# Loading a decoder kernel's weights first: the small parameters wait behind eight weight pieces, and the first activations are fetched inside the setup

## The reference

```python
x = _layernorm(x + _L0_attn_ref(x, ...))       # attention through 16 "splat" centres per head
x = _layernorm(x + _L0_xattn_ref(x, ctx, ...)) # attention to 120 context tokens
x = _layernorm(x + _L0_ffn_ref(x, ...))        # best one of 8 experts, 256 x 256 each
x = _layernorm(x + _L1_attn_ref(x, ...))       # causal attention
x = _layernorm(x + _L1_xattn_ref(x, ctx, ...)) # two attention blocks, each with a 256-1024-256 MLP
x = _layernorm(x + _L1_ffn_ref(x, ...))        # best 4 of 16 experts of 64 hidden features
```

## Time and profile before

| | |
|---|---|
| time, median of 3 runs | 3904.42 us (3902.85 to 9488.8; the middle one of the three is the median) |
| the profiled execution | 3903.38 us, its span 3901.6 us |
| PE busy | 3338.3 us, 86% of the span |
| DVE busy | 2759.7 us, 71% |
| ACT busy | 2093.8 us, 54% |
| POOL busy | 971.6 us, 25% |
| first instruction of the PE | 71.51 us after the start of the span |

### The profile page before, as it was taken

How to read it: one execution, slowest core, us unless ns; L and a number is a source line. 1 busy time by engine, 2 the same in 40 slices (tenths; PEclk the granted TensorE clock), 3 DMA queues, 4 the chain that set the end, 5 groups by cost and what they waited for, 6 DMA issues and landing times. The chain is left out here.

```text
span 3901.6 us, 94561 instructions
## 1 busy us (share of the span) xinstructions
PE 3338.3 (86%) x38960; PEld 2367.8 (61%) x38960; DVE 2759.7 (71%) x6299; ACT 2093.8 (54%) x4222; POOL 971.6 (25%) x1792
## 2 busy tenths in 40 slices
PE   1899888988898888988988888899888898988886
PEld 1666565666565656656656666576656665755654
DVE  5777676777776767767767667677776677767655
ACT  4745565455556564554465555545555556455552
POOL 0312341122222321131133122212342112124310
PEclk9989898989899989989889888899988998988887
DMA  5000000000000000000000000000000000000000
GB/s 165 3 3 2 2 3 5 9 8 3 2 2 3 6 3 7 7 3 2 7 2 2 5 4 8 5 4 2 2 2 3 10 9 4 2 2 2 1 4 6
DMA packets 30365, 31.49 MB, mean 8 GB/s; under 512 B 8673, under 2 KB 26482, under 8 KB 29938
## 3 DMA queue, kind: packets, MB, share of 16 engines
q1 hardware_dynamic: 29938, 25.44, 2.1%
HBM read 21.24 MB, written 4.19 MB: 7 GB/s over the span
## 5 line engine op out<-in xcount | busy, mean ns | idle before, releaser
L1113 ACT ACTIVATE p<-bank,p_log 128x512 f32<-128x512 f32 (+2 forms) x1280 | 746.5, 583 | 1299.2 <-PE bank L805 1242.7
L1687 POOL TENSOR_TENSOR prob<-p,prob 120x256 f16<-120x256 f32 (+2 forms) x512 | 452.4, 884 | 1746.5 <-ACT prob L1114 1745.0
L1114 ACT ACTIVATE prob<-bank,p_log 128x512 f16<-128x512 f32 (+2 forms) x1280 | 746.8, 583 | 0.0
L1389 DVE TENSOR_REDUCE negm<-bank 128x2 f16<-128x512 f32 (+1 forms) x1280 | 674.5, 568 | 30.5 <-PE bank L760 19.4
L1307 DVE TENSOR_TENSOR prob<-p,prob 128x512 f16<-128x512 f32 (+2 forms) x768 | 469.6, 618 | 181.8 <-ACT prob L1114 177.1
L782 PE MATMUL bank<-q,k 32*128 32x256 f16 (+2 forms) x6144 | 491.0, 286 | 59.2 <-issue 20.1
L672 PE MATMUL bank<-w_exp,ident_h 128*128 128x512 f16 x1280 | 426.6, 418 | 20.9 <-DVE k L1328 8.5
L1696 POOL TENSOR_SCALAR_AFFINE_SELECT probm<-prob 128x128 f16<-128x128 f16 x1024 | 325.6, 359 | 335.4 <-DVE prob L1307 335.1
L782 PEld LDWEIGHTS bank<-q,k 32*128 32x128 f16 (+1 forms) x6144 | 306.1, 109 | 137.4 <-issue 55.6
L805 PE MATMUL bank<-ident_h,negm 128*128 128x256 f16 (+2 forms) x2560 | 379.0, 270 | 0.0
L850 PE MATMUL bank<-v,prob 128*128 128x17 f16 (+2 forms) x8448 | 328.3, 174 | 33.3 <-DVE prob L1307 20.7
(11 more groups left out here) (302 smaller groups left out, 6254.8 us busy)
## 6 DMA issues: line engine op xcount, KB each, us to landing
x<-in_x SPq DMA_DIRECT2D x16, 256.0 KB, 2.7
out<-z SPq DMA_DIRECT2D x16, 256.0 KB, 2.2
xa<-in_li SPq DMA_DIRECT2D x9, 256.0 KB, 4.2
x<-in_li SPq DMA_DIRECT2D x7, 256.0 KB, 4.6
z<-in_wq SPq DMA_DIRECT2D x4, 256.0 KB, 4.1
z<-in_li SPq DMA_DIRECT2D x4, 256.0 KB, 4.6
cx<-in_ctx_t SPq DMA_DIRECT2D x16, 60.0 KB, 2.2
cx<-in_ctx SPq DMA_DIRECT2D x16, 60.0 KB, 1.8
```

Of the source, the lines that this page charges most:

```text
L1113: act(p32[0:n, g % PBUF32, 0:cols], ps[0:n, 0:cols], ACT.Exp, bias=p_log[0:n, :], scale=a.scale)
L1114: act(prob[0:n, 0, g % PBUF, 0:cols], ps[0:n, 0:cols], ACT.Exp, bias=p_log[0:n, :], scale=a.scale).then_inc(a_done, one(a_done))
L1389: v.tensor_reduce(negm[:, h * NT:(h + 1) * NT], ring_v[bank_of(e, v_full)][:, :].rearrange("p (t n) -> p t n", t=NT)[:, :, 0:ATTNS[k].keys ...
L1687: g.tensor_tensor(prob[0:n, 1, m % PBUF, 0:cols], p32[0:n, m % PBUF32, 0:cols], prob[0:n, 0, m % PBUF, 0:cols], ALU.subtract).then_inc(pp_ ...
```

## The change: pieces first, constants in the middle, x inside the setup

Four things are changed, all of them in the setup block or at the seam between the blocks:

1. SP issues weight pieces 0 to 7 first, then the 18 parameters of group 0 (now `needed`), then the rest of the pieces. The 17 of group 1 (`needed_later`) are issued one behind every second piece, from piece 8 to piece 40.
2. ACT makes the high parts of pieces 0 to 7 before it waits for group 0 and runs the two `exp`. DVE makes the low parts of pieces 0 to 7 before the constants.
3. The buffers are assigned from the end: piece n uses buffer (n - 61) % 8, so that the last pieces in `x` are 53, 54 and 55 and not 56, 57 and 58.
4. The first three `x` and context transfers are issued at the end of the setup's SP program, each `x` as soon as `low_made` says that its buffer is free, and not after the barrier.

No computing instruction is added or taken away. The diff, cut:

```diff
-        buffers = x + xa + z
+        def place_of(n):
+
+            return (n - len(chunks)) % STAGING
...
-                load(e, 0, cen[:, 0], io["centers"].rearrange("(t p) d -> p t d", p=P))
...
-                for n, (_, src, tiles, cols) in enumerate(chunks):
-                    if n >= STAGING:
-                        e.wait_ge(low_made, n + 1 - STAGING)
-                    e.dma_start(staging(n, tiles, cols), src).then_inc(staged[n % STAGING], 16)
+                def stage(n):
+                    _, src, tiles, cols = chunks[n]
+                    if n >= STAGING:
+                        e.wait_ge(low_made, n + 1 - STAGING)
+                    e.dma_start(staging(n, tiles, cols), src).then_inc(staged[place_of(n)], 16)
...
+                for n in range(STAGING):
+                    stage(n)
+                for dst, src in needed:
+                    load(e, 0, dst, src)
+                for n in range(STAGING, len(chunks)):
+                    stage(n)
+                    if needed_later and n % 2 == 0:
+                        load(e, 1, *needed_later.pop(0))
+                for dst, src in needed_later:
+                    load(e, 1, dst, src)
+                for b in range(LANES):
+                    e.wait_ge(low_made, len(chunks) - STAGING + LANE[b] + 1)
+                    e.dma_start(x[LANE[b]][:, :, :], io["x"][b].rearrange("(t p) f -> p t f", p=P)).then_inc(
+                        x_in[LANE[b]], 16)
+                for b in range(LANES):
+                    e.dma_start(cxT[LANE[b]], io["ctx_t"][b]).then_inc(c_in[LANE[b]], 16)
...
-                e.wait_ge(w_ready[0], w_count[0])
-
-                nc.scalar.activation(s_small[:, 6:10], s_small[:, 0:4], ACT.Exp).then_inc(s_act, 1)
-                nc.scalar.activation(s_small[:, 10:11], s_small[:, 4:5], ACT.Exp, scale=-1.0).then_inc(s_act, 1)
                 for n, (parts, _, tiles, cols) in enumerate(chunks):
-                    e.wait_ge(staged[n % STAGING], 16 * (n // STAGING + 1))
+                    if n == STAGING:
+                        e.wait_ge(w_ready[0], w_count[0])
+                        nc.scalar.activation(s_small[:, 6:10], s_small[:, 0:4], ACT.Exp).then_inc(s_act, 1)
...
                 for n, (parts, _, tiles, cols) in enumerate(chunks):
-                    e.wait_ge(staged[n % STAGING], 16 * (n // STAGING + 1))
+                    if n == STAGING:
+                        constants()
+                    e.wait_ge(staged[place_of(n)], 16 * (n // STAGING + 1))
                     e.wait_ge(high_made, n + 1)
...
-                for b in range(LANES):
-                    fetch_x(b)
-                for b in range(LANES):
-                    fetch_ctx_t(b)
```

More of the change, by code:

```diff
@@ L400, in spread_row @@
             return ap.rearrange("(a n) -> a n", a=1).broadcast_to([P, ap.shape[0]])
-        buffers = x + xa + z
+        def place_of(n):
+            return (n - len(chunks)) % STAGING
         def staging(n, tiles, cols):
-            flat = buffers[n % STAGING][:, :, :].rearrange("p a b -> p (a b)")
+            flat = (x + xa + z)[place_of(n)][:, :, :].rearrange("p a b -> p (a b)")
             return flat[:, 0:tiles * cols].rearrange("p (a b) -> p a b", b=cols)
@@ L451, in _ @@
-                load(e, 1, r_route[:, :], spread_row(io["route"]))
+                def stage(n):
[3 more added lines that the diff above has]
+                    e.dma_start(staging(n, tiles, cols), src).then_inc(staged[place_of(n)], 16)
+                needed = [
+                    (cen[:, 0], io["centers"].rearrange("(t p) d -> p t d", p=P)),
+                    (cen[:, 1], io["centers_t"].rearrange("(t p) d -> p t d", p=P)),
+                    (dlt[:, 0], io["deltas"].rearrange("(t p) d -> p t d", p=P)),
+                    (dlt[:, 1], io["deltas_t"].rearrange("(t p) d -> p t d", p=P)),
+                    (s_small[:, 0:2], io["log_scales"]),
+                    (s_small[:, 2:4], io["log_amps"]),
+                    (s_small[:, 4:5], spread_row(io["movement"])),
+                    (s_small[:, 5:6], spread_row(io["temperature"])),
+                    (p32[0:EXPERTS, 1, 0:DM], io["expert_b"])]
@@ new lines, in _ @@
+                for r, name in enumerate(("bo2", "li1_b0", "li1_b1", "li3_b0", "li3_b1")):
+                    needed.append((p32[BROW + r:BROW + r + 1, 0, 0:DM], io[name].rearrange("(a n) -> a n", a=1)))
+                for a in range(2):
+                    for c, name in enumerate(("ln_g", "ln_b")):
+                        needed.append((p32[GROW + a:GROW + a + 1, 0, c * DM:(c + 1) * DM],
+                                       io[f"{name}{a}"].rearrange("(a n) -> a n", a=1)))
+                needed_later = [(r_router[:, :], spread_row(io["router_b"])), (bq2[:, :], io["bqkv2"]),
+                                (r_route[:, :], spread_row(io["route"]))]
@@ L454, in _ @@
                                      (g3, "ln3_g"), (b3, "ln3_b"), (b_li2, "li2_b")):
[L455 to L458, removed]
-                for n, (_, src, tiles, cols) in enumerate(chunks):
-                    if n >= STAGING:
-                        e.wait_ge(low_made, n + 1 - STAGING)
-                    e.dma_start(staging(n, tiles, cols), src).then_inc(staged[n % STAGING], 16)
+                        needed_later.append((dst[a][:, :], io[f"{src}{a}"]))
+                for n in range(STAGING):
[14 more added lines that the diff above has]
+                    e.dma_start(cxT[LANE[b]], io["ctx_t"][b]).then_inc(c_in[LANE[b]], 16)
                 e.wait_ge(w_ready[0], w_count[0])
@@ L562, in _ @@
-                for o in range(2):
-                    step(v.tensor_reduce(parity[:, o:o + 1], block16[:, o::2, 0], AX.X, ALU.add))
-                    step(v.tensor_scalar(k_scale[:, o], s_small[:, 8:10], parity[:, o:o + 1], None, ALU.mult))
-                step(v.tensor_scalar(cen[:, 1], cen[:, 1], -2.0, None, ALU.mult))
-                for t in range(KT):
-                    step(v.tensor_tensor(minus2c[:, t].rearrange("p (h s) -> p h s", s=16), block16[:, :, :],
-                                         cen[:, 1, t:t + 1, :].broadcast_to([P, 8, 16]), ALU.mult))
```

77 lines of the change are left out of this document (41 added, 36 removed).

## The result

| | before | after |
|---|---|---|
| time, median of 22 runs | 3898.17 us | 3888.39 us (3871.36 to 3898.41) |
| ratio | | 0.9969, 95% interval 0.9958 to 0.9979 |
| span of the profiled execution | 3901.6 us | 3886.9 us |
| first instruction of the PE | 71.51 us | 60.92 us |
| from there to the end of the span | 3830.1 us | 3826.0 us |

The ratio is of means, and one run of the kernel before, of 9488.8 us, is left out of it as a slow one. Times 3898.17 us it makes 12.1 us less, with an interval from 8.2 to 16.4 (the two medians are 9.8 us apart); the prediction's sum was 12.0. The interval leaves out 1: small as it is, this is a change that was measured.

A forecast was written before the change was run, and what follows sets the result against it. The setup was taken as bound in turn by SP's issuing, DVE's constants and the DMA engines. Moving the PE's start from 71.51 to 59.5 us took 12.0 off 3903.38, giving 3891.4, stated as 3892.0 us, range 3887 to 3898.

The forecast's parts named there:

- The chain of the setup: Setup: SP's issuing, DVE's constants and the DMA-bound pieces decide the PE's start, which comes 12.0 us earlier.
- What a measurement can tell: Whole kernel: 0.3% less, where about 2% can be told from no change; 0.98 on a time within 2%.
- the text's own cases: Whole kernel: forecast 0.78, later PE start or delayed parameters 0.10, main-part loss 0.07, choked stream 0.03, larger gain 0.02.
- The rest of the pieces: Setup behind the constants: 42.01 us less seven full pieces at 0.73 us each gives 36.9 us, ending at 58.3.
- Group 1: Thirteen small parameter loads among pieces 16 to 40 cost 0.06 us of the DMA engines each, 0.8 us together.
- The rival's place: Pieces 16 to 40: group 1 loads choke the stream, 24.7 us in place of 0.8, 12 us slower; chance 0.03.
- x inside: End of the setup: x issued before the barrier leaves 0.4 us of the 3.15 us between DVE's end and PE's start.
- The cover: Last pieces: x has some 1.86 us before the last low part and needs 0.73, so it is there at the barrier.
- The seam: Between the blocks: PE starts 0.4 us behind DVE; the rival of a later start, by x or code fetch, gives 3893 to 3895.
- The rule on issuing: Setup: by the skill, issue order is worth next to nothing; the prediction set 35 issues in 14.9 us against it.
- The main part: From PE's start on: same length within 2 us; the rival of a 4 to 12 us loss there had 0.07.

The follow-up runs named there:

- the cuts: Kernels with the second block reduced to the wait for lane 1's x, four transpositions and one small output transfer; setup before 77.06 us, changed 66.09 us.
- the order: Changed kernel with the first x and contexts issued behind the barrier as before; ratio 0.9978 to the kernel before, setup timed alone 68.90 us.
- group 1 on GpSimd: Changed kernel with the 17 group 1 loads issued by GpSimd behind its own constants, none by SP; ratio 0.9963 to the kernel before.
- the cut with no group 1: Changed kernel's setup timed without the decoder, the 17 group 1 loads left out altogether; 64.76 us against 65.27 us on the same chip.
- Thin spreading: Group 1 on GpSimd, plus 13 DVE constant operations ahead of piece 8 and 17 ahead of every third piece; setup 63.09 us, whole kernel 3869.03 us.
- evenly spread constants: Group 1 on GpSimd, plus one DVE constant operation ahead of each piece from 8 on; ratio 0.9962 to the kernel before.

## Why the prediction was right, and where not

**The chain of the setup: right.** That the PE's start decides, that SP's issuing, DVE's constants and the DMA-bound stream are its three pieces, holds: each joint up to 21.43 us came within 0.06 us. The size of the whole, 12.0 us, is inside the measured 8.2 to 16.4. That it is so near to 12.1 is luck: the PE's start moved by 10.6 us in the profiles and by 10.3 in the cuts. The time, 3888.39 us, is inside the range of 3887 to 3898 but just below the forecast's 3889 to 3895. The reason is the starting point: the sum was taken from 3903 to 3904 us, and the median of 22 runs of the kernel before is 3898.17.

**What a measurement can tell: wrong.** This is the step that failed: "0.3% less, where about 2% is what a measurement of this kernel can tell from no change", and with it the forecast of a time that can't be told from no change. The repeated runs give the ratio to within 0.11% on either side, so 0.3% is well told from nothing. The 0.98 on a time within 2% was right about 2% and said nothing of the question that was open here, whether it gets faster at all. On that the text's own cases put over 0.9 on the faster side. The mistake was to take a width of 78 us for the noise when its own table had two runs 1.6 us apart.

**The rest of the pieces, 36.9 us: too short.** In the setups timed alone the order's PE start is 68.90 - 5.34 = 63.6 us, where the terms give 59.1 + 3.15 = 62.3. Since group 1 was dearer in the sum (0.8) than by the medians (0.5), the stretch of the 45 pieces itself is about 1.6 us longer. The term took seven pieces at 0.73 us each off the 42.01 us and left the rest as it was. The refill behind the constants did not stay as it was. These are the windows from 3 to 9 us behind the first full transfer, in the kernel before, the changed one, the one with group 1 on GpSimd, and the cut with no group 1:

```profile
29.35:35.35 6.00, 0.00 (x0) 0.00 (x0) 4.72 (x9) 4.65 (x8) 0.00 (x0) 1.00 1.05 344
24.43:30.43 6.00, 0.00 (x0) 0.00 (x0) 3.87 (x8) 3.01 (x7) 0.00 (x0) 1.00 0.84 240
24.43:30.43 6.00, 0.00 (x0) 0.00 (x0) 5.42 (x10) 4.43 (x9) 0.00 (x0) 1.00 0.98 317
24.43:30.43 6.00, 0.00 (x0) 0.00 (x0) 4.83 (x9) 3.44 (x7) 0.00 (x0) 1.00 0.83 271
```

The changed kernel gets 104 GB/s less for 6 us, which at 358 GB/s is 1.7 us (an estimate); in the 30 us behind, the two run at 350 and 344. So the missing time sits at the restart. Group 1 on SP can be a part of it only, since 271 GB/s without it is low too. What else is new there: pieces 18 and 20, with half of the bytes for one issue each, now come among the first five behind the constants and not behind nine others. That they cost the rest was not tested. Thin spreading fills the pause and got about 1.7 us back, but the kernel before has that pause too, so it does not explain the difference.

**Group 1, 0.8 us: right in size, its resource not shown.** It was priced as time of the DMA engines, and the cuts put 0.5 to 0.8 us on it without telling the engines from SP's queue. The sentence beside it, that SP has 1.43 us of issues in every 1.46, names what bound the stream once there was one load more for two pieces. The rival's place was right, though its price (24.7 us) came from landing times, and the queue took 5.8 us for 17 loads more.

**x inside, 2.75 us: 2.2.** The cover was right: the PE waited for the barrier, 0.32 us behind DVE. The 0.5 us less is at the edge of what the runs tell. In the whole kernels' profiles the low parts end 0.8 us later with x inside, in those of the cuts at the same time (68.67 both) and 0.4 earlier (60.37 against 60.73). Whether x costs the last pieces anything stays open.

**The seam: right.** The PE had nothing else left to wait for, and began 0.32 us behind DVE's last instruction; no stall for code is seen. The Trainium skill's rule in "Runtime: NRT & Kernel Launch", "Instruction fetch mechanics", is on taken branches to a target outside the two-page window. Whether this branch is one is not on record, so the trace does not speak against the rule.

**The rule on issuing.** "DMA: Bandwidth & Descriptors", "Issuing engines are not separate DMA queues", says in the Trainium skill that sequencer time is usually small beside the DMA. For this kernel's small loads the trace agrees on one of them alone, 0.43 to 0.47 us of SP against 1.9 us from issue to landing, but not on many in a row: there the 0.47 us of SP stand against 0.06 us of the engines, and the queue is what they cost.

**The main part: no loss,** as forecast. The distance from the PE's start to the end is 4.1 us shorter, which is more than the 2 us that the prediction allowed, with a granted clock of 0.904 against 0.900. At equal clock the order alone has -8.9 us where its PE starts 8.6 us earlier, and GpSimd's variant -12.5 where it starts 13.7 earlier; in the other seven variants the time at equal clock fell by 0.9 to 3.1 us more than the PE's start moved in the one profile.

## What to carry to other kernels

In this kernel, transfers that were many and tiny were priced by the queue that issued them, not by the bytes: set the issue times for one big transfer and the small ones beside it (0.96 us with one small load for each, 0.73 with one for every two) against the time that the engines need for the big one (0.73). When loads are reordered, write the chain out joint by joint; rows gave each within 0.06 us here, up to the first stretch where a resource is shared. And before a small difference between two profiles is explained, cut the program to the part in question and time that: here the profiles said 3.1 us where repeated timing said 0.5 to 0.8.

## What the runs showed of the hardware

The time of the whole kernel goes with the mean granted clock of TensorE from run to run. Two of the runs of the kernel with evenly spread constants took 3856.37 us at a clock of 0.916 and 3897.83 at 0.897: 41.5 us for 0.019, or 2.2 us for each 0.001. Over the 35 runs of the kernel before on each of two chips the correlation is -0.97, with slopes of 2.5 and 2.2 us. The clock is the likely reason why the profiled run of after was 14.7 us shorter with a PE start only 10.6 us earlier: its PE is busy 0.42% less for the same matmuls, and its clock of 0.904 is 0.44% above 0.900. Taking the clock out leaves a standard deviation of 1.7 and 2.3 us in place of 6.2 and 9.3. One of the changed kernel's 22 runs does not follow: at a clock of 0.869 it took 3893.72 us, where three others at 0.900 took 3891.56 to 3893.31. What makes the chip grant more or less clock in one run was not tested.

GpSimd issued the same small loads at one every 0.53 us, close to SP's 0.47, on a queue that had nothing else to do.
